# Gap matmuls, one group's maxima spread by TensorE, four weight products on GpSimd, and an earlier turn of the gates in an attention and FFN kernel

## What is computed

```
x1  = concat(q, k, v)
ig, fg = x1 @ Wi + bi, x1 @ Wf + bf                # gates of each head and position
log_D[s,t] = cum(log_sigmoid(fg))[s] - cum(...)[t] + ig[t]   for t <= s
D   = exp(log_D - max_t log_D)                     # maxima of each head and row
C   = (q k^T / sqrt(32)) * D
h   = C / (max(|sum C|, exp(-max)) + 1e-6) @ v
x   = x + groupnorm(h) * ln_scale
```

```
gate, up = layernorm(x) @ W_gu^T        # 2 x 1408 rows
y  = (silu(gate) * up) @ W_down^T       # 1408 -> 512
x  = x + y / sqrt(mean(y*y) + 1e-6)
```

## Time and profile before

| | us |
|---|---|
| median of three runs | 517.07 |
| the three runs | 510.53, 518.31, 517.07 |
| the profiled execution | 513.8 |
| its span, by the trace | 512.0 |

### The profile page before, as it was taken

The page is one execution under the profiler, slowest core; times in us unless marked ns, Lnnn a source line. Parts: engine busy times, 40 slices in busy tenths (PEclk is TensorE's granted clock), DMA queues, the critical chain, the costliest instruction groups (busy, mean ns, idle before and its releaser), DMA issues.

```text
span 512.0 us, 8396 instructions
## 1 busy us (share of the span) xinstructions
PE 488.4 (95%) x2839; PEld 292.2 (57%) x2839; DVE 382.8 (75%) x688; ACT 299.1 (58%) x648; POOL 322.0 (63%) x368
## 2 busy tenths in 40 slices
PE   8999999689999999999999999999999989999996
PEld 3678866347776445477774445477774444444442
DVE  4878899758888999278888998478888952999411
ACT  1858754578886344588876234788874123877210
POOL 3034465067877772678877883678868661999610
PEclk9999999889999999999999999999999999999999
DMA  8967040273004100464006001572000000200011
GB/s 245 276 238 280 1 165 2 53 270 140 36 2 175 73 1 3 169 238 170 2 13 237 0 1 44 205 254 77 2 1 2 20 20 22 102 1 1 0 43 41
DMA packets 15804, 46.39 MB, mean 91 GB/s; under 512 B 1680, under 2 KB 1808, under 8 KB 14608
## 3 DMA queue, kind: packets, MB, share of 16 engines
q1 hardware_dynamic: 15760, 45.84, 25.7%
HBM read 37.31 MB, written 4.33 MB: 81 GB/s over the span
## 4 chain that ended last, share of the span: by engine, by line
PE 75%; DVE 12%; ACT 4%; DMA 3%; issue 3%; POOL 2%; SPq 0%; POOLq 0%; DVEq 0%; ACTq 0%
PE pf L1157 19%; PE pf L1093 19%; PE pf L1131 7%; PE pq L960 7%; PE po L1022 5%; PE pq L1116 3%; PE pf L1116 3%; ACT dmat L710 2%; DMA negm<-negm_dram 2%; PE pq L900 1%; PE po L993 1%; PE pf L1176 1%; PE pq L1093 1%; PE po L1116 1%; DMA ffn<-in_x 1%
## 5 line engine op out<-in xcount | busy, mean ns | idle before, releaser
L568 POOL TENSOR_TENSOR ffn<-ffn,ts 128x512 f32<-128x512 f32 x88 | 118.1, 1347 | 38.5 <-DVE ffn L1457 35.6
L1093 PE MATMUL pf<-yT,gu_val 128*128 128x512 f16 x464 | 136.7, 384 | 3.8 <-ACT ts L744 2.1
L1157 PE MATMUL pf<-w_down,hT 128*128 128x512 f32 x264 | 115.8, 595 | 0.0
L744 ACT ACTIVATE ts<-pf,gu_scale 128x512 f32<-128x512 f32 x134 | 85.1, 683 | 10.9 <-PE pf L1093 5.9
L1157 PEld LDWEIGHTS pf<-w_down,hT 128*128 128x128 f32 x264 | 49.3, 190 | 60.6 <-issue 57.2
L710 ACT ACTIVATE dmat<-negm,aT 128x128 f32<-128x128 f32 x248 | 77.5, 392 | 4.4 <-DMA negm<-negm_dram 4.4
L1093 PEld LDWEIGHTS pf<-yT,gu_val 128*128 128x128 f16 x464 | 56.3, 128 | 35.8 <-DVE ffn L1457 3.6
L527 POOL TENSOR_SCALAR_AFFINE_SELECT dmat<-dmat 128x512 f32<-128x512 f32 x64 | 41.5, 661 | 46.8 <-ACT dmat L710 46.7
L573 POOL TENSOR_TENSOR hT<-ffn,th 128x512 f32<-128x512 f32 x44 | 57.8, 1317 | 16.4 <-DVE th L1465 16.4
L1022 PEld LDWEIGHTS po<-v_sb,dmat 128*128 128x128 f32 x384 | 63.1, 191 | 4.6
L1022 PE MATMUL po<-v_sb,dmat 128*128 128x33 f32 x384 | 58.3, 233 | 0.0
(11 more groups left out here) (158 smaller groups left out, 767.0 us busy)
## 6 DMA issues: line engine op xcount, KB each, us to landing
negm<-negm_dram SPq DMA_DIRECT2D x31, 512.0 KB, 6.2
xT<-in_ctx_T SPq DMA_DIRECT2D x4, 1024.0 KB, 7.4
ctx_sb<-in_ctx SPq DMA_DIRECT2D x4, 1024.0 KB, 5.3
x_sb<-in_x SPq DMA_DIRECT2D x4, 1024.0 KB, 5.8
x_res<-x_sb SPq DMA_DIRECT2D x4, 1024.0 KB, 4.8
out<-x_res SPq DMA_DIRECT2D x16, 256.0 KB, 2.1
ffn<-in_x SPq DMA_DIRECT2D x3, 1024.0 KB, 9.4
ts<-in_gate_up_bytes SPq DMA_DIRECT2D x4, 352.0 KB, 9.4
```

What stands on the lines that cost most here:

```text
L568: pool.tensor_tensor(acc, acc, ts[:, h % TDEEP, 1], ALU.add).then_inc(tsum_ready, 1)
L744: act.activation(ts[:, h % TDEEP, g], bank(q, h, g), ACT.Copy, scale=gu_scale[:, g * GU + o:g * GU + o + 1]).then_inc(t_ready, 1)
L1093: ins = pe.matmul(bank(q, h, g), gu_val[:, h // 2 + h % 2 * FT, g], yT[:, part, g], start=(part == 0), stop=(part == 1))
L1157: last = pe.matmul(pf[:, tt], hT[:, j, tt * P:(tt + 1) * P], w_down[:, j], start=(j == 0), stop=(j == FT - 1))
```

## The change

- `EPS_DOWN`: the down weights lose their factor of 64; the norm behind them uses an epsilon divided by 64 squared.
- GpSimd makes four of the eleven down weight tiles (`POOL_WEIGHTS`: tile 7 behind h = 9, 8 behind h = 11, 9 and 10 behind h = 14), DVE the other seven, and DVE's decoding is moved: `decode_down(3)` and tile 0 behind unit 3.
- For pair 0, unit 1 gets its maxima from PE too (`spread_rows(1, ...)`, into `po` and `pq[:, 1]`), not by DMA.
- Fillers: 2, 1 and 2 around the scores of unit 0 in place of 4 and 6; 6 in units 2 and 3 in place of 8; 19 behind `centre_v` in place of 16; 8 new ones behind `turn_y` in the first iteration.
- `turn_back(1)` moves from behind the up tile h = 0 to between its second and third group; DVE reads it ahead of that tile's sums.
- `head_sums` of batch 0 moves one step earlier, to h = 16.

```diff
+EPS_DOWN = EPS / 64.0 ** 2
+POOL_WEIGHTS = {9: (7,), 11: (8,), 14: (9, 10)}
...
+        def bank_rows(u, half):
+            return pf[:, 2 * half + 1] if u == 0 else pq[:, 1] if half else po[:]
...
-                load_units(range(1, 4))
+                load_units(range(1 if p else 2, 4))
...
+            def down_weights(j):
+
+                pool.wait_ge(s_dsc, 16)
+                pool.wait_ge(dn4_ready, DOWN_CHUNKS)
+                pool.tensor_tensor(w_down[:, j], dn_fp4[:, j], dn_by[:, j], ALU.mult).then_inc(pool_wd, 1)
...
                     if q is None and h == 14:
                         rstd1(n)
+                    if q is None and h in POOL_WEIGHTS:
+                        for j in POOL_WEIGHTS[h]:
+                            down_weights(j)
...
-                if p == 0 and u == 0:
-                    act.wait_ge(bc_done, half + 1)
+                if p == 0 and u < 2:
+                    act.wait_ge(bc_done, 2 * u + half + 1)
...
-            act.wait_ge(wd_ready, FT)
+            act.wait_ge(wd_ready, FT - 4)
+            act.wait_ge(pool_wd, 4)
...
-                if u < 2:
-                    pe.wait_ge(v_ready, 2 * u + 2)
-                if u > 0:
+                if u == 0:
+                    pe.wait_ge(v_ready, TT)
+                    pe.wait_ge(exp_done, 4)
+                else:
                     pe.wait_ge(o_read, u)
...
-                    if k < 6 or u < 4:
+                    if k < 6 or u < 2:
                         keep_busy(1)
...
                 for g in range(KT):
                     if q == 0 and h == 1 and g == 3:
                         pe.wait_ge(floor_ready, 4)
+                    if q == 0 and h == 0 and g == 2:
+                        turn_back(1)
...
-            def spread_first(half):
-
-                if half == 0:
-                    pe.wait_ge(nm_ready, 1)
+            def spread_rows(u, half):
+
                 for hh in range(2):
-                    r = 2 * half + hh
-                    last = pe.matmul(pf[:, 2 * half + 1, hh * S:(hh + 1) * S],
+                    r = u * DH + 2 * half + hh
+                    last = pe.matmul(bank_rows(u, half)[:, hh * S:(hh + 1) * S],
                                      ident[0:ROWS, r:r + 1].to_broadcast([ROWS, P]), nm[:], start=True, stop=True)
                 last.then_inc(bc_done, 1)
...
-                    if q == 0 and h == 0:
-                        turn_back(p)
...
                             scores(p, q, SCORES[s], 0)
-                            keep_busy(4, po[:])
+                            keep_busy(2, pf[:, 2])
+                            spread_rows(1, 0)
+                            keep_busy(1, pf[:, 2])
                             scores(p, q, SCORES[s], 1)
-                            keep_busy(6, po[:])
+                            keep_busy(2, pf[:, 2])
+                            spread_rows(1, 1)
                             state_sums(p, q, SCORES[s])
...
                         centre_v(n)
-                        keep_busy(16)
+                        keep_busy(19)
...
                     turn_y(p)
+                if q is None:
+                    keep_busy(8)
...
-                elif u < 3:
-                    decode_down(2 * u - 2)
-                    decode_down(2 * u - 1)
+                elif u == 1:
+                    decode_down(0)
+                    decode_down(1)
+                elif u == 2:
+                    decode_down(2)
+                elif u == 3:
+                    decode_down(3)
+                    down_weights(0)
+                elif u < UNITS - 1:
+                    down_weights(2 * u - 7)
+                    down_weights(2 * u - 6)
                 else:
-                    if u == UNITS - 1:
-                        shift1(1)
-                    for j in range(2 * u - 6, 2 * u - 4 if u < UNITS - 1 else FT):
-                        down_weights(j)
+                    shift1(1)
...
                     if q is not None:
-                        ffn_up(q, h, p, u)
                         if q == 0 and h == 0:
                             read_a(p)
+                        ffn_up(q, h, p, u)
...
-                    if q is None and h == 17:
+                    if q is None and h == 16:
                         head_sums(p, 0)
```

More of the change, by code:

```diff
@@ L265, in xattn_ffn @@
         wd_ready = sem("wd_ready")
+        pool_wd = sem("pool_wd")
         waits_taken = sem("waits_taken")
@@ L578, in down_scale @@
                 c = slice(tt, tt + 1)
-                pool.tensor_scalar(ms[:, c], ssq[:, c], 1.0 / E, EPS, ALU.mult, ALU.add).then_inc(ms_ready, 1)
+                pool.tensor_scalar(ms[:, c], ssq[:, c], 1.0 / E, EPS_DOWN, ALU.mult, ALU.add).then_inc(ms_ready, 1)
                 pool.wait_ge(ms_ready, TT * q + tt + 1)
@@ L693, in exps @@
                 hg, b = u // 2, u % 2
-                if p == 0 and u == 0:
-                    act.wait_ge(bc_done, half + 1)
+                if p == 0 and u < 2:
+                    act.wait_ge(bc_done, 2 * u + half + 1)
                 elif half == 0:
-                    spread = 2 * p + u // 4 + 1 - (u % 4 == 0)
+                    spread = 2 * p + u // 4 + 1 - (u % 4 < 2)
                     act.wait_ge(s_negm[u % 4], 16 * spread)
@@ L707, in exps @@
                     bh = b * DH + hg * HG + h
-                    m = pf[:, 2 * half + 1, hh * S:(hh + 1) * S] if p == 0 and u == 0 else negm[:, u % 4, h]
+                    m = bank_rows(u, half)[:, hh * S:(hh + 1) * S] if p == 0 and u < 2 else negm[:, u % 4, h]
                     for c in range(BLKS):
@@ L1149, in down @@
                     if q == 0:
-                        pe.wait_ge(wd_ready, FT)
+                        pe.wait_ge(wd_ready, FT - 4)
+                        pe.wait_ge(pool_wd, 4)
                     pe.wait_ge(t_ready, 4 * FT * (q + 1) - 2)
@@ L1237, in _ @@
             keep_busy(4)
-            spread_first(0)
+            pe.wait_ge(nm_ready, 1)
+            spread_rows(0, 0)
             turn_back(0)
-            spread_first(1)
+            spread_rows(0, 1)
             keep_busy(2, pf[:, 2])
@@ L1525, in down_weights @@
                     dve.wait_ge(s_dsc, 16)
-                dve.scalar_tensor_tensor(w_down[:, j], dn_fp4[:, j], FP4_SCALE, dn_by[:, j],
+                dve.scalar_tensor_tensor(w_down[:, j], dn_fp4[:, j], 1.0, dn_by[:, j],
                                          ALU.mult, ALU.mult).then_inc(wd_ready, 1)
```

## The result

| | before | after |
|---|---|---|
| median, 22 executions each | 513.54 us | 516.5 us |
| lowest and highest | 510.53, 521.31 | 513.7, 517.8 |
| profiled execution | 513.8 us | 516.71 us |
| its span | 512.0 us | 515.0 us |
| mean granted clock of PE in it | 0.993 | 0.993 |

The ratio is 1.005, with a 95% interval of 1.003 to 1.007: the change made the kernel slower, by 1.5 to 3.6 us. That is inside the 2% forecast and inside the stated range, but I had forecast no change.

A forecast was written before the change was run, and what follows sets the result against it. PE bounds from 105.4 us; before that a chain through PE, DVE, DMA and ACT. Terms 0.95 - 0.26 - 0.69 - 0.1 + 0.3 - 0.3 = -0.1 us turned 515.4 into 515.3 us, range 509.8 to 518.8 us.

The forecast's parts named there:

- Base: Starting time for the sum: 515.4 us, the middle of four executions including the profiled one.
- rival (c): GpSimd's products 9 and 10 hold up DVE's adds of units 6 and 7: slower, 516.9 us; chance 0.22.
- Unit 1's maxima by PE: Unit 0 on PE: two added spreading pairs less five saved fillers make PE later, +0.95 us.
- Rival (d): DVE and ACT, not PE, pace units 0 to 3, so earlier exponentials carry through: 514.3 us; chance 0.08.
- Fillers and the stall: PE in units 2 and 3: fewer fillers give -0.26 us, unit 3 without its stall -0.69 us.
- head_sums one step earlier: DVE and ACT behind unit 7: second head sum ends at 73.8 to 74.3 us against 73.95, taken as -0.1 us.
- contention: GpSimd's products 9 and 10 stretch DVE's add of unit 6: +0.3 us, bounds 0 and 1.08 us.
- GpSimd's four products: Four weight products moved from DVE to GpSimd, priced at 1.3 us each, change the total by 0.0 us.
- The cover that I gave as 3.9 us: Slack between by_ln_scale ending near 75.4 us on GpSimd and DVE wanting its first tile at 79.07 us.
- Turn of the gates and fillers: PE before h = 3: h = 0 runs at 2.4 GHz, idle time grows to about 3.5 us; 0.0 us.
- Clock: Slow clock around h = 3 may come and end sooner, while PE idles: -0.3 us, bounds 0.3 lost, 1.7 gained.
- rival (b): Clock falls vanish or land in the idle time before h = 3: 1.7 us shorter, 513.7 us; chance 0.25.

The follow-up runs named there:

- b_head: Kernel before with only head_sums of batch 0 moved to h = 16; ratio 1.0007 to the kernel before.
- b_spread: Kernel before with only unit 1's maxima by PE and 2, 1 and 2 fillers around unit 0's scores; ratio 1.0024 to the kernel before.
- u_head: Changed kernel with head_sums of batch 0 back at h = 17; ratio 0.9996 to the kernel before.
- u_pool: Changed kernel with all eleven weight products and the decoding order of before on DVE; ratio 1.0038 to the kernel before.
- u_sh: Changed kernel with unit 1's maxima by DMA, fillers 4 and 6, and head_sums of batch 0 at h = 17; ratio 0.9988 to the kernel before.
- s_nofill: Changed kernel with head_sums at h = 17 and without the five fillers around unit 0's scores; ratio 1.0011 to the kernel before.
- best2: u_sh with ACT emptying h = 2 before the exponentials, and 6 fillers, not 8, in units 0 and 1; ratio 0.9891 to the kernel before, profiled execution 531.13 us.

## Why the prediction was wrong, step by step

**Base.** 515.4 us was the middle of four executions; the median of 22 is 513.5. Three executions of a kernel that spreads by 8 us were the weakest number of the sum. I took the spread for unexplained; about half of it goes with the granted clock, which the 40 slices of the page show. That 516.5 lies close to the 516.9 of rival (c) is luck: the base was 1.9 us too high, and the change of 3.0 us is more than any of the four cases held.

**Unit 1's maxima by PE, +0.95 us predicted.** Right in mechanism, 1.24 us in size, and confirmed by doing and undoing it. A pair takes 1.06 us and not 1.03, and five fillers spread over three places save less than 5 x 0.22: 2.27 us of fillers became 1.38, since each group has about 0.1 us of its own. The wait of unit 0's values for unit 1's exponentials costs nothing, as put: they end at 34.97 us and the values start at 35.57. Rival (d) is dead.

**Fillers and the stall, -0.26 and -0.69 us predicted.** Measured 4.94 - 4.73 = 0.21 and 5.37 - 4.77 = 0.60 us. Not all of the second is the change's: in b_head and b_spread, whose program there is that of the kernel before, unit 3 takes 5.17 us and unit 4 4.78. What I had missed is unit 4 (4.81 us instead of 4.68 in the profile before) and 0.1 us in unit 0 (5.05 instead of 4.94). Unit 5's state sums wait for its `vw`, which takes 0.98 us under two weight products of DVE. The decoding that I counted as "moved, hence free" made DVE later: its add in unit 4 now starts 0.02 us behind a mask of GpSimd instead of 0.33 us ahead of it, takes 0.75 us instead of 0.30, and pushes the products against `vw`. Together that leaves +0.68 us at unit 7, where I had 0.0; this zero is the second step that failed.

**head_sums one step earlier, -0.1 us predicted: the step that failed.** It costs 1.14 us (done alone 1.13). I had the right list of what stands behind one another, and priced it at 73.8 to 74.3 us against 73.95 before. Two things went wrong. The add of unit 7 takes 1.04 us and not 0.3 to 0.8: later part and add together 1.35 us, where I had 0.6 to 1.1. It runs beside `by_ln_scale` on GpSimd, and single instructions of the traces tell what sets its length (us):

| kernel | add starts | GpSimd's instruction that runs then ends | add ends |
|---|---|---|---|
| before | 70.80 | 71.46 | 71.61 |
| b_head | 70.94 | 71.67 | 71.83 |
| after | 72.32 | 73.21 | 73.37 |
| u_head | 70.85 | 71.02 | 71.17 |
| u_pool | 72.25 | 72.98 | 73.13 |

The add isn't slowed, it waits for the end of that one instruction. This holds for all 99 adds of `later` that start under a GpSimd instruction in the fourteen traces: each ends 0.14 to 0.16 us behind it, the 1.359 us of the earlier trace rows included, and the others take 0.28 to 0.30 us. So the price hangs on the moment at which the add comes. I had put the contention (+0.3 us) on the add of unit 6; it fell on that of unit 7. And I held the sum against the end in the kernel before, 73.95 us. With the weight products gone from DVE and the old order kept, the stretch behind unit 7 is 3.12 us (u_head, and 3.13 in u_sh), so that end would have been 73.5. The unloading of DVE brought 0.49 us in the old order (3.61 to 3.12) and 0.47 us in the new (4.74 to 4.27), and the reordering took back more than twice that. In the old order it came by way of GpSimd: with no product of DVE beside it the first instruction of `by_ln_scale` takes 1.17 us instead of 1.68, and lets the add through 0.5 us sooner. In the old order ACT's squares of batch 1 lie under a head sum of DVE; in the new one each waits for the other.

**GpSimd's four products, 0.0 us, and contention, +0.3 us predicted.** The price of one, 1.10 us against my 1.3, was near. They gain 0.47 us behind unit 7 and lose 0.4 us behind the head sums; net nothing. Rival (c), that they hold up the adds, didn't come true: the add of unit 6 takes 0.33 us. That is luck of the moment: it starts at 69.35 us, and the product under way ends at 69.52. What they did hold up is a small product of DVE (1.06 us instead of 0.16; it starts at 69.60 and ends at 70.66 us, GpSimd's product ends at 70.63), which stood in nobody's way. The cover that I gave as 3.9 us is 3.7 by my own numbers (79.07 - 75.4); nothing hung on it. The Trainium skill's sentence on the shared interfaces of GpSimd and VectorE (GPSIMD Engine Reference, Specifications) agrees with these 1.06 us and with the 0.98 us of `vw`; as a forecast for the total it would have been wrong. In the prediction I said that the add's median of 0.284 us disagrees with it; that was misread, since those adds start while no GpSimd instruction runs.

**Turn of the gates and fillers, 0.0 us predicted.** Right in what I said of the path: h = 0 runs at 2.4 GHz, PE's idle time before h = 3 grows (3.09 us against 2.10), and h = 3 doesn't start sooner for it. What I had undervalued is the other side: slow transposes are on the path, and they cost 1.0 us in the one profile without these fillers.

**Clock, -0.3 us predicted, rival (b) -1.7.** The profiled execution of the changed kernel has a slow stretch of 6.8 us at h = 3, not a shorter one. Over all its executions the clock is no worse than before (0.9924 and 0.9956 in two sets, before 0.9921 on three chips), so nothing speaks for it as a cause of the loss. Rival (b) named the right place with the wrong cure: it is worth 3.5 us (2.3 at equal clock), but PE has to get work there, and fillers ahead of y's tile don't give it any. That nothing but ACT's program order made h = 3 wait was in my own description of the chain, and I didn't draw the conclusion from it.

What stays open: the cause of the pause of 0.5 us on DVE in the statistics of x, whether the delay of b_head reaches the end in full, and why the loss at equal clock (2.7 us) is larger than that at h = 3 (1.8 and 2.25 us).

## What to carry to other kernels

Hold each edit against the kernel as the other edits leave it, not against the kernel before: the 73.95 us that I compared the new order with would have been 73.5 in the old one. That is the smaller part; the new order costs 1.13 us in the kernel before as well (b_head). Where two engines hand a job to each other twice (squares, sums, squares, sums), keep the second squares under the first sums, even if an engine then sits idle ahead of them. And where the most loaded engine waits at a fixed place, look first at what stands ahead of its releaser in that engine's program: moving one condition gave 3.5 us, more than any other part. An instruction of VectorE that comes while GpSimd is in the middle of one can wait for all the rest of it, so the moment counts: in unit 4 a shift of 0.35 us cost the add 0.45.

## What the runs showed of the hardware

- PE can be busy all the time and still fall to 1.2 GHz: on spreads of 48 rows and scores of 32 rows at 33 us (s_nofill, 0.50 from 34 to 38 us, PE 1.93 to 2.00 us busy in every 2). In one execution with fewer fillers it fell at 39.3 us, 1.9 us behind a wait of 0.86 us, and stayed down until 87.1 us with PE busy for 19.87 of 20 us (best2). Which property of the work decides is not shown.
- The granted clock goes with about half of the spread between executions: 515.9 us up to a mean clock of 0.991, 512.4 us from 0.995 on (before, 74 of 93 executions).
- GpSimd's product of an fp8 and an f16 tile of 128x512 to f32 takes 1.10 us, less than its sum of two f32 tiles (1.27 us), while DVE takes 0.78 us.
- A DVE product of 128x4 elements took 1.06 us instead of 0.16 us: it started under a 128x512 product of GpSimd and ended 0.03 us behind it.
- A DVE add of two SBUF tiles of 128x132 that starts while a GpSimd instruction runs ends 0.14 to 0.16 us behind the end of that instruction, whatever is left of it (99 of 99 in fourteen traces, 0.32 to 1.36 us long); alone it takes 0.28 to 0.30 us.
